# Keys, queries and attention values moved into the gather stage, and every other bucket's tile 1 fetched row by row

## The reference

```
h      = relu(layernorm(x))
dots   = sum((h[src] @ K.T) * relations[rel] * (h[src] @ Q.T)) / 128
values = exp(dots)                               # depends on (src, rel) alone
values = values / segment_sum(values, by (src, rel))
msgs   = values * h[dst]
output = segment_sum(msgs, by (rel, src))
out    = x + relu(sum over r of W_r @ output[r]),   W = comps x bases
```

## Time and profile before

| | |
|---|---|
| median of 3 runs | 3081.46 us (3079.8 to 3084.72) |
| profiled execution's own time | 3066.26 us |
| its span | 3064.5 us |
| mean granted TensorE clock | 0.673 of full speed |
| busy in the span | PE 51%, DVE 44%, ACT 15%, POOL 54% |
| gather stage | first gather starts at 421.6 us, bucket 48's first gather at 2995.6 us |

### The profile page before, as it was taken

The page is one execution under the profiler, slowest core; times in us unless marked ns, Lnnn a source line. Parts: engine busy times, 40 slices in busy tenths (PEclk is TensorE's granted clock), DMA queues, the critical chain, the costliest instruction groups (busy, mean ns, idle before and its releaser), DMA issues.

```text
span 3064.5 us, 32426 instructions
## 1 busy us (share of the span) xinstructions
PE 1549.4 (51%) x9121; PEld 1129.2 (37%) x9122; DVE 1354.7 (44%) x2385; ACT 462.7 (15%) x918; POOL 1651.2 (54%) x1804
## 2 busy tenths in 40 slices
PE   4999932444344454534454443544444444544435
PEld 3666621233233333323333332333333333333324
DVE  7999934334243433424343342434334243433423
ACT  4666611000010100001010000101000010101000
POOL 3444444655646465555646565564655556464653
PEclk8999965656666665666666566666656566666667
DMA  5444411111111111111111111111111111111111
GB/s 154 156 155 155 155 55 32 46 41 42 45 36 45 36 46 39 43 42 41 45 36 45 38 44 43 40 45 37 45 38 43 44 39 45 36 46 36 45 42 29
DMA packets 99825, 170.47 MB, mean 56 GB/s; under 512 B 32491, under 2 KB 48612, under 8 KB 99575
## 3 DMA queue, kind: packets, MB, share of 16 engines
q0 software_dynamic: 51776, 104.48, 13.1%
q1 hardware_dynamic: 47672, 65.57, 6.3%
q10 hardware_dynamic: 352, 0.14, 0.0%
HBM read 112.24 MB, written 59.59 MB: 56 GB/s over the span
## 4 chain that ended last, share of the span: by engine, by line
another core or an unknown queue 40%; issue 21%; DVE 20%; PE 14%; SPq 2%; DMA 2%; DVEq 1%; ACT 0%; POOLq 0%; ACTq 0%
PE bank L1199 6%; DVE arena L825 4%; DVE CX L790 3%; PE bank L1184 2%; DVE stage L768 2%; DVE WC L801 2%; DVE pay_all L784 1%; PE bank L1152 1%; PE bank L1276 1%; DVE OHR L766 1%; PE bank L1319 1%; DMA RL<-bucket_streams 1%; DVE pay_all L815 1%; PE bank L1307 1%
## 5 line engine op out<-in xcount | busy, mean ns | idle before, releaser
L492 POOL DMA_INDIRECT arena<-Z_messages,IDX x1568 | 1483.0, 946 | 1137.4 <-issue 955.1
L1319 PE MATMUL bank<-arena 128*128 128x128 f32 x3528 | 695.2, 353 | 733.1 <-issue 724.9
L1319 PEld LDWEIGHTS bank<-arena 128*128 128x128 f32 x3528 | 632.5, 264 | 797.3 <-issue 795.3
L799 DVE TENSOR_SCALAR WC<-bank 128x128 f32<-128x128 f32 x49 | 14.3, 292 | 1150.5 <-remote 1149.2
L1101 ACT COPY pay_all<-bank 128x1024 bf16<-128x1024 bf16 x147 | 108.0, 807 | 2136.6 <-remote 2059.9
L1307 PE MATMUL bank<-pay_all 128*128 128x256 bf16 x882 | 179.8, 347 | 310.9 <-DVE arena L825 249.1
L825 DVE TENSOR_TENSOR arena<-stage,bank 128x512 f32<-128x512 bf16 x441 | 268.9, 681 | 12.1 <-remote 7.8
L768 DVE TENSOR_TENSOR stage<-bank,NLF 128x4608 bf16<-128x4608 f32 x49 | 242.4, 4948 | 0.0
L1307 PEld LDWEIGHTS bank<-pay_all 128*128 128x128 bf16 x882 | 86.6, 113 | 386.2 <-DVE arena L825 297.4
L1276 PE MATMUL bank<-stage,OHR 128*128 128x512 bf16 (+1 forms) x441 | 198.5, 618 | 3.2 <-DVE arena L825 3.1
L1199 PE MATMUL bank<-WT,HT 128*128 128x512 f32 x392 | 186.3, 615 | 0.0
(11 more groups left out here) (211 smaller groups left out, 1715.5 us busy)
## 6 DMA issues: line engine op xcount, KB each, us to landing
Z_messages<-stage SPq DMA_DIRECT2D x192, 256.0 KB
arena<-Z_messages,IDX POOLq DMA_INDIRECT x1568
X<-in_x SPq DMA_DIRECT2D x4, 768.0 KB, 12.8
out<-O SPq DMA_DIRECT2D x48, 64.0 KB
bucket_streams<-bucket_streams SPq DMA_DIRECT2D x97, 18.0 KB
arena<-in_L_gnn_bases_w SPq DMA_DIRECT2D x1, 1024.0 KB, 15.0
bucket_streams<-arena SPq DMA_DIRECT2D x1, 882.0 KB
RL<-bucket_streams SPq DMA_DIRECT2D x49, 18.0 KB
```

The lines of the kernel that those rows point to most:

```text
L492: g.indirect_dma_start(Gbuf[par][:, k, :], None, Z, bass.IndirectOffsetOnAxis(IDX[turn][:, k:k + 1], 0))\
L1319: return t_.matmul(bank[2][:, 0:EMB], OW[:, k, :], Gbuf[par][:, k, :], start=start, stop=stop)
```

## The change

In words:

- **Stream stage.** `keys_queries`, `copy_so`, `key_query`, the `relT` matmul and the Exp are gone from the steps.
- **Gather stage, values.** In the step of bucket b these are made for bucket b+1: DVE `value_normalise` (H), PE `value_turn` (transpose into bank 2), DVE `value_relu`, PE `value_keys` (two float32 matmuls into bank 2), DVE `value_product` (a copy and a product), PE `value_dots`, ACT `value_exp`. Bank 2 also holds the sums of `aggregate`, so aggregate(b-1) now waits for the exp of bucket b+1 (`v`), and value_turn waits for `o`.
- **Gather stage, tile 1 of odd buckets.** POOL leaves out tile `ROWK`=1. SP loads that tile's record row (`load_one`), DVE makes 128 row numbers of it (ONEZ), and `single_rows` fetches the 128 rows of Z one by one: rows 32 to 127 by SP, rows 0 to 31 by ACT, each by a DMA of its own (512 bytes), with one register load for every 8 rows. The semaphore `row` holds up PE's `aggregate` and ACT's `shared_tile` of odd buckets until all rows are there.
- **Order.** SP no longer stores outputs and no longer waits for RL, and does both joins at once; its rows for bucket b-2 come after the loads of bucket b. ACT stores outputs, and shares a tile one step later than before.

The core of the diff:

```diff
+                def load_one(b, turn, m):
+                    if dyn(b) or m >= 1:
+                        sp.wait_ge(s["onez"], m * 2 - 1)
+                        sp.sem_inc(s["sp_go"], 1)
+                    row = sp.value_load(ROWI[0:1, bass.ds(b + 5 * NB + 1, 1)], min_val=0, max_val=(TOP + E) // P)
+                    sp.dma_start(ONER[turn][:], stream[bass.ds(row + ROWK, 1), :]).then_inc(oner[turn], 16)
+
+                def single_rows(b, turn, m):
+                    sp.wait_ge(s["onez"], m * 2 + 2)
+                    sp.sem_inc(s["sp_go"], 1)
+                    if dyn(b) or b >= 3:
+                        sp.wait_ge(s["acc"], b - 1)
+                        sp.wait_ge(s["shared"], b - 1)
+                    sp.sem_inc(s["sp_go"], 1)
+                    for p in range(ACTROWS, P, 8):
+                        _, rows = nc.values_load_multi_w_load_instructions(
+                            ONEZ[turn][:, 1, p:p + 8], engines=[mybir.EngineType.SP], min_val=0, max_val=ZROWS - 1,
...
+                        for k in range(8):
+                            sp.dma_start(Gbuf[1][p + k:p + k + 1, ROWK, :], Z[bass.ds(rows[k], 1), :]).then_inc(s["row"], 16)
...
+                    load_records(b, par)
+                    if par == 1:
+                        load_one(b, turn, m)
+                    if par == 1 and (dyn(b) or b >= 3):
+                        single_rows(b - 2, 1 - turn, m - 1)
...
                     for k in range(FIRSTK, FLOOR):
-                        tile(k)
+                        if par == 0 or k != ROWK:
+                            tile(k)
                     tail(FLOOR)
...
+            def value_product(b):
+                dve.wait_ge(s["nkq"], b + 1)
+                if dyn(b) or b >= 1:
+                    dve.wait_ge(s["npr"], b)
+                v.tensor_copy(SO[:, 0:P], NKQ[:, P:2 * P]).then_inc(s["nq"], 1)
+                dve.wait_ge(s["nq"], b + 1)
+                if dyn(b) or b >= 1:
+                    dve.wait_ge(s["nv"], b)
+                v.tensor_tensor(PR[0][:], NKQ[:, 0:P], SO[:, 0:P], ALU.mult).then_inc(s["npr"], 1)
...
                     if dyn(b) or b < NB:
                         own_counts(b)
+                    if dyn(b) or b + 1 < NB:
+                        value_product(b + 1)
+                    if dyn(b) or b < NB:
                         weights(b, par)
...
                     if dyn(b) or b + 1 < NB:
+                        value_exp(b + 1)
                         spread_relations(b + 1, 1 - par)
-                        shared_tile(b, par)
-
+                    if dyn(b) or b >= 1:
+                        shared_tile(b - 1, 1 - par, m * ROWS)
+                    if dyn(b) or b >= 2:
+                        store_out(b - 2, par)
+                    if par == 1:
+                        single_rows(b, turn, m)
...
                     if dyn(b) or b >= 1:
                         pe.wait_ge(s["o"], b)
+
+                    if dyn(b) or b + 2 < NB:
+                        pe.wait_ge(s["v"], b + 3)
```

More of the change, by code:

```diff
@@ L187, in program @@
         IDX = [sb(f"IDX{p}", [P, G], I32) for p in range(4)]
+        ONER = [sb(f"ONER{p}", [1, P], F32) for p in range(2)]
+        ONEZ = [sb(f"ONEZ{p}", [1, 2, P], I32) for p in range(2)]
         NLI = sb("NLI", [P, 2, G], I32)
@@ new lines, in _ @@
+                join(0, 1)
+                bucket(0, 0)
+                bucket(1, 1, 0, 0)
+                with sp.Fori(0, (NB - 3) // 4) as j:
+                    bucket(j * 4 + 2, 0)
+                    bucket(j * 4 + 3, 1, 1, j * 2 + 1)
+                    bucket(j * 4 + 4, 0)
+                    bucket(j * 4 + 5, 1, 0, j * 2 + 2)
+                for b in range(2 + (NB - 3) // 4 * 4, NB):
+                    bucket(b, b % 2, b // 2 % 2, b // 2)
+                single_rows(NB - 2, (NB - 2) // 2 % 2, (NB - 2) // 2)
@@ L1080, in spread_relations, with store_out, single_rows, shared_tile @@
                     a.copy(ORD[:], OHR[par][:].unsqueeze(2).broadcast_to([P, G, 4, R])).then_inc(s["ord"], 1)
-                def shared_tile(b, par):
+                def store_out(b, par, n=P):
+                    act.wait_ge(s["o"], b + 1)
+                    act.sem_inc(s["act_go"], 1)
+                    a.dma_start(out[bass.ds(b * P, n), :], O[par][0:n, :]).then_inc(ost[par], 16)
+                def single_rows(b, turn, m):
+                    act.wait_ge(s["onez"], m * 2 + 2)
+                    act.sem_inc(s["act_go"], 1)
+                    if dyn(b) or b >= 3:
+                        act.wait_ge(s["acc"], b - 1)
+                        act.wait_ge(s["shared"], b - 1)
+                    act.sem_inc(s["act_go"], 1)
+                    for p in range(0, ACTROWS, 8):
+                        _, rows = nc.values_load_multi_w_load_instructions(
+                            ONEZ[turn][:, 1, p:p + 8], engines=[mybir.EngineType.Activation], min_val=0, max_val=ZROWS - 1,
+                            skip_runtime_bounds_check_because="a record holds a row of Z or the empty row")
+                        for k in range(8):
+                            a.dma_start(Gbuf[1][p + k:p + k + 1, ROWK, :], Z[bass.ds(rows[k], 1), :]).then_inc(s["row"], 16)
+                def shared_tile(b, par, row_total):
                     last = act.value_load(ROWI[0:1, bass.ds(b + 6 * NB + 1, 1)], min_val=0, max_val=G - 1)
@@ L1254, in _, with value_turn, value_keys, value_dots @@
             pe.wait_ge(s["rec_sb"], NCH)
-            pe.wait_ge(s["v"], NCH)
             bad = pe.value_load(ROWI[0:1, 3 * NB:3 * NB + 1], min_val=0, max_val=16 * NB)
+            NHT = bank[2][:, P:2 * P]
+            NKQ = bank[2][:, 2 * P:4 * P]
+            NV = bank[2][:, P:P + R]
+            def value_turn(b, free):
+                pe.wait_ge(s["nh"], b + 1)
+                if dyn(b) or b >= 1:
+                    pe.wait_ge(s["v"], b)
+                if free is not None:
+                    pe.wait_ge(s["o"], free)
+                t_.transpose(NHT, H[:], identf[:]).then_inc(s["nth"], 1)
+            def value_keys(b):
+                pe.wait_ge(s["nht"], b + 1)
+                t_.matmul(NKQ[:, 0:P], KQT[:, 0, :], HT[0][:], start=True, stop=True)
+                t_.matmul(NKQ[:, P:2 * P], KQT[:, 1, :], HT[0][:], start=True, stop=True).then_inc(s["nkq"], 1)
+            def value_dots(b):
+                pe.wait_ge(s["npr"], b + 1)
+                t_.matmul(NV, PR[0][:], relT[:], start=True, stop=True).then_inc(s["nv"], 1)
             with pe.If(bad < 1):
@@ L1290, in sum_counts @@
                 def sum_counts(b):
[L1291 removed]
+                    pe.wait_ge(s["v"], b + 1)
                     pe.wait_ge(s["cx"], b + 1)
```

186 lines of the change are left out of this document (105 added, 81 removed).

## The result

The change makes the kernel slower: 3757.7 us (median of 4 runs, 3754.91 to 3760.72) against 3080.63 us for the kernel before (4 runs, 3078.38 to 3084.72), a ratio of 1.2196 with a 95% interval of 1.2175 to 1.2217. The profiled execution took 3760.72 us, its span is 3759.0. The prediction was 3745.

The account below looks back on a forecast made before the run. It took a chain of waits in the gather stage as the bound, and SP's rows after the change. 3066.3 - 16 (stream stage) + 667 (rows) + 10 (first and last buckets) = 3727, as a median 3745 us; range 3250 to 4200.

Parts of the forecast that it names:

- What bounds the kernel: Gather stage: a chain of waits sets the pace, no engine being full; period 53.8 us by its sum, 53.5 measured.
- my chain: Gather stage, per bucket: 38.8 us of gathers, 6.5 to the release, 7.7 of sums, 0.8 to POOL's next gather.
- Stream stage: Steps before the gathers: PE loses matmul entries, DVE becomes the bound after 0.36 us a step; -16 us, bounds 0 and -17.
- Value chain: Gather stage: aggregate waits for the moved value work and does all 72 sums after the release; +4.9 us a bucket.
- Rows: SP's 96 single-row DMAs per odd bucket outlast the gathers; a pair takes 136 us against 107, +667 in all.
- release: Gather stage: moment when waiting engines are let go, 6.5 us after POOL's last gather of a bucket.
- slow pace: SP's queue from about 8 us into a gather: 0.7 us or more per entry, 4.2 us per row.
- free stretch: SP's time before the slow pace: 8.8 us in the first gather of a pair, half used by joins, 7 rows.
- the first two buckets: Value chains of the first and last buckets in the forecast's sum, +10 us.
- B: Rival: SP keeps up, rows are hidden and only the value chain costs; 3265 us, or 3400 with ACT's 6 us; chance 0.15.
- C: Rival: one cause makes late sight and slow pace, and the change may remove it; -45 us, median 3036; chance 0.09.
- late sight: Gather stage: DVE and ACT see PE's finished results only at the release, 6.6 us after POOL's last gather.

Follow-up runs that it names:

- e2: Changed kernel with the value work put back in the stream stage, single rows kept; 2363.86 us, 0.9877 of the kernel before (2393.69 us).
- e12: The kernel of e1 again (values moved, no single rows), run beside the unedited changed kernel; 3267.66 us, 1.066 of the kernel before (3067.61 us).
- e7: Changed kernel, single rows kept, with the PE order of e3; 2338.62 us, 0.9762 of the kernel before (2395.38 us).
- e1: Changed kernel without single rows, GpSimd fetching tile 1 of odd buckets again, values still moved; 2367.21 us, 0.989 of the kernel before (2393.69 us).
- e5: Changed kernel with SP's rows read from fixed addresses, one queue entry each, no register loads; 2340.1 us, 0.9767 of the kernel before (2395.38 us).
- e3: e1 with keys and queries in bank 0 behind the sums of counts, dots in bank 5 behind aggregate; 2367.42 us, 0.9892 of the kernel before.
- e4: Changed kernel with rows 80 to 127 of odd buckets' tile 1 not fetched, so SP has 48 rows, not 96; 2337.31 us, 0.9765 of the kernel before.

## Why the prediction was right, point by point

- *What bounds the kernel.* Right for the condition in which the kernels were compared: in the new trace too, DVE's copy starts 6.1 to 7.0 us after the last gather's start in each of the buckets 2 to 47, and SP's entries are slow. What I took for a property of the kernel is a condition under which it ran. Under the other one GpSimd's gathers are the bound, and nothing of my chain exists.
- *Stream stage*, forecast -16 us. The first gather starts at 395.25 in place of 421.64: -26.4, outside the bounds of 0 and -17 as well. The mechanism was right (DVE becomes the bound), the size off. DVE's pitch went from 6.90 us (L655, 49 steps from 56.8 to 394.9) to 6.37 (L670, 56.8 to 368.9), 0.53 us a step, not 0.34. I had let DVE's own work stand, but one of its operations got shorter as well: the one-hot compare, before

```profile
L563 DVE TENSOR_TENSOR OHB<-iotaB,q 125x1600 f16<-125x1600 f16 x40 | 43.8, 1096 | 0.0
```

and after

```profile
L578 DVE TENSOR_TENSOR OHB<-iotaB,q 125x1600 f16<-125x1600 f16 x41 | 40.0, 977 | 0.0
```

  With the value work back in this stage (e2) the same compare (L587) takes 1089 ns again, so the longer time goes with that work. That it is GpSimd's `key_query` fits, since in the trace before its 0.9 us start 0.5 us into the compare (199.87 and 199.36 in one step), but no run takes `key_query` away by itself.
- *Value chain*, forecast +4.9 us a bucket with no gather saved. In e12 buckets 2 to 48 start 516.7 to 3199.4, 58.3 us apart against 53.5: **+4.8**. In the bucket shown the dots come 0.7 us behind DVE's copy and aggregate 1.8 behind it (2.5 in the changed kernel's second aggregate above; forecast 2.6). Over 46 buckets of e12 the sums take 10.4 us (forecast 10.0), and from the start of POOL's last gather of a bucket to the next bucket's first it is 19.6 us in place of 14.7. e12's 200 us against a sum of 48 x 4.8 - 26 = 204 closes.
- *Rows.* Forecast: a pair of buckets takes 136 us in place of 107. Buckets 2 to 48 of the changed kernel start at 518.01 and 3668.27: 137.0 a pair. The inside of the sum was less good. Mean over 22 odd buckets: 11 rows before the first release (17 forecast), 32 between it and the next slow pace (37), 10.5 in it (10), 42 behind the second release (32), in 21.5 us (20), if the slow pace is taken to begin 8 us into a gather, as in the forecast. A row out of gathers cost 0.51 us with its share of the loads, less than my 0.57. Against that, the free stretch before them, up to 8 us into the gather, gave 0.9 rows in place of 7: SP was at its joins, and the first row came 12.2 us behind the gather's start on average. Two errors of opposite sign. Two more terms were off: the slow pace was there 3 us into the second gather on average (the first entry of L354 over 0.6 us), not 8; and the 2 us for a row's landing, behind which no row stood, were 1.2 in the pair shown (1948.8 to 1950.0). ACT's rows did run at SP's slow pace, which the prediction had left open. They hold up ACT's copies in every second bucket, to 8.5 to 12.5 us behind the last gather's start, and this is hidden, since aggregate then waits for SP's rows still longer.
- *Sum.* 3759.0 - 3064.5 = 694.5 us: -26.4 to the first gather, +9.9 for the first two buckets, +689 for 46 periods, +22 behind the start of bucket 48's first gather, where the last rows and the last sums are not overlapped. Forecast were -16, +10, +667 and nothing for the end, 661 in all. That the medians came as close as 3745 and 3757.7 is in part luck: 18 us of the forecast were the 0.5% by which the median lay above the profiled run before, and with the changed kernel it lay 3 us below it.
- *Rivals.* B's condition (SP keeps up) held in no run of the stalled condition; its value chain did (3265 forecast, e12 3267.66, which has no rows at all). C said that the late sight and the slow pace have one cause and might vanish, to give 45 us: in the free condition they are gone together and e7 gains 56.8. So C was the right picture of the other condition, for a cause that I had not named: not PE's position in the program, since e1 and e12 are one program.
- *Open.* What makes a core stalled: the runs show only that it isn't the program, nor a fixed trait of the chip, if a number stands for one chip (11 and 14 were each met in both conditions). A trait of a single core, or what else ran on the chip, is not excluded: neither is on record. No run changes the condition at will, so that the slow entries and the late sight have one cause is inferred from their coming and going together. Whether rows and values add up there (e2), the price of an entry against that of a DMA (e5), and whether e3's order heals the value chain there: these kernels met the free condition only. The changed kernel itself was not met in the free condition; e4, e5 and e7, each near to it, take 0.976 or 0.977 of the kernel before.

## What to carry to other kernels

When a trace shows events seen late by several engines at once and register moves of 0.7 us, time the unchanged kernel again at another time before building on it: one change cost 22% and, as nearly the same program, gained 2.4%, according to a condition that the unchanged kernel showed just as well. Work that an engine starts in many small entries, such as 96 single rows of three entries, is cheap only while its queue runs freely; in the stalled traces the register entries pay as the DMA entry does, and so does each wait for another engine's result that is added to the path behind the stall. Compared by what each can lose, 2.4% free (read from e7, the nearest kernel met there) against 22% stalled, the kernel before is the safer of the two.

## What the runs showed that I had not expected

The same program takes 2366 or 3268 us (e1, e12), steady to 0.1% and 0.3% within a set of runs, on a chip of the same number at different times. In the stalled condition SP's and ACT's queue entries take some 0.7 us and up to 1.4 while GpSimd starts gathers, and return to 0.03 to 0.23 us some 6.5 us after its last one; the events of PE that DVE's copy and ACT's copies wait for are seen only then too; the gathers themselves keep their 1.25 us in both. And the gather's 1.25 us hardly depends on its rows: 64 in place of 128 save 0.03.
